# One more 128-column product per chunk in the weighted sum pass of a graph network kernel

## What is computed

```python
msgs = x[edge_src] * edge_val[:, None]
agg = jax.ops.segment_sum(msgs, edge_dst, num_segments=x.shape[0])
return agg @ weight
...
x = x + _L1_gnn_ref(_layernorm(x, axis=-1), src, dst, edge_weight, L1_gnn_weight)
```

## Time and profile before

| | us |
|---|---|
| median of 3 runs | 4542.22 |
| lowest and highest | 4536.57, 4546.24 |
| span of the profiled execution | 4528.2 |
| TensorE matmul busy in it | 3398.2 (75%) |
| POOL busy | 2322.5 (51%) |
| DVE busy | 2037.4 (45%) |
| ACT busy | 1546.8 (34%) |

### The profile page before, as it was taken

The page is one execution under the profiler, slowest core; times in us unless marked ns, Lnnn a source line. Parts: engine busy times, 40 slices in busy tenths (PEclk is TensorE's granted clock), DMA queues, the critical chain, the costliest instruction groups (busy, mean ns, idle before and its releaser), DMA issues. The chain is left out here.

```text
span 4528.2 us, 63030 instructions
## 1 busy us (share of the span) xinstructions
PE 3398.2 (75%) x18888; PEld 2727.4 (60%) x18888; DVE 2037.4 (45%) x5783; ACT 1546.8 (34%) x4091; POOL 2322.5 (51%) x2298
## 2 busy tenths in 40 slices
PE   3777887614396777774577199999778999998796
PEld 3555555412164555553466199998436888887696
DVE  4666555650144444342422311113445777777523
ACT  3554555310132222221322122222125666665432
POOL 3454555447405565554466543442336877875153
PEclk7788888756697887786789599999789999999698
DMA  6765555100005666661355377775549999997476
GB/s 188 217 168 149 153 159 146 53 22 3 0 24 191 223 226 212 205 219 49 94 166 157 101 243 246 248 235 165 142 150 244 268 261 268 266 265 188 136 214 206
DMA packets 491983, 777.53 MB, mean 172 GB/s; under 512 B 154330, under 2 KB 296995, under 8 KB 491395
## 3 DMA queue, kind: packets, MB, share of 16 engines
q1 hardware_dynamic: 359986, 498.14, 35.0%
q0 software_dynamic: 122608, 266.94, 23.8%
q10 hardware_dynamic: 9056, 8.43, 0.6%
HBM read 599.88 MB, written 173.38 MB: 171 GB/s over the span
## 5 line engine op out<-in xcount | busy, mean ns | idle before, releaser
L875 POOL DMA_INDIRECT sum_rows<-t_row,src_i x416 | 394.5, 948 | 441.1 <-POOLq L2144 161.2
L875 POOL DMA_INDIRECT ag_rows<-t_att,src_i x416 | 401.2, 964 | 372.9 <-DVE ag_msg L986 253.8
L1746 POOL DMA_INDIRECT eg_early<-t_edge,src_i x312 | 486.6, 1560 | 167.0 <-issue 90.2
L286 POOL DMA_INDIRECT t_cells<-times_seen,cell x416 | 405.5, 975 | 263.9 <-issue 126.7
L1066 PE MATMUL ps<-featT,ag_msg 128*128 128x128 f32 x1664 | 365.6, 353 | 131.8 <-issue 117.8
L1794 PE MATMUL ps<-eg_w,eg_rT 128*128 128x256 f32 x1664 | 434.4, 384 | 0.0
L1066 PEld LDWEIGHTS ps<-featT,ag_msg 128*128 128x128 f32 x1664 | 275.4, 236 | 232.2 <-issue 187.7
L1114 PE MATMUL ps<-sum_w1g,sum_eaT 64*128 64x256 f32 x1248 | 242.0, 521 | 203.7 <-ACT sum_kept L1158 117.8
L1473 PE MATMUL ps<-cv_cells,cv_high 128*128 128x384 f32 (+2 forms) x1200 | 323.2, 350 | 91.4 <-DMA cv_cells<-t_cells 91.4
L972 DVE TENSOR_TENSOR att_sums<-att_sums,ps 128x384 f32 x416 | 228.6, 550 | 310.7 <-remote 128.9
L1177 DVE TENSOR_TENSOR featT<-featT,ps 128x256 f32 x416 | 175.3, 421 | 401.4 <-remote 230.1
(11 more groups left out here) (446 smaller groups left out, 6746.8 us busy)
## 6 DMA issues: line engine op xcount, KB each, us to landing
cv_cells<-t_cells SPq DMA_DIRECT2D x225, 384.0 KB
t_pre<-sum_kept SPq DMA_DIRECT2D x156, 512.0 KB
eg_early<-t_pre SPq DMA_DIRECT2D x156, 512.0 KB
t_cells<-zeros SPq DMA_DIRECT2D x21, 1664.0 KB
cv_cells<-t_cells SPq DMA_DIRECT2D x75, 448.0 KB
xn<-in_L_ffn_W SPq DMA_DIRECT2D x57, 512.0 KB
xn<-in_L_ffn_expert_w SPq DMA_DIRECT2D x110, 256.0 KB
ag_trow<-t_dst SPq DMA_DIRECT2D x104, 256.0 KB
```

The lines of the kernel that those rows point to most:

```text
L286: nc.gpsimd.indirect_dma_start(out=t_cells, out_offset=bass.IndirectOffsetOnAxis(ap=cell[:, c:c + 1], axis=0), in_=times_seen[:, c:c + 1], ...
L875: nc.gpsimd.indirect_dma_start(out=rows[:, j, :], out_offset=None, in_=table, in_offset=bass.IndirectOffsetOnAxis(ap=src_i[:, n:n + 1], ax ...
L1746: nc.gpsimd.indirect_dma_start(out=early[:, q % ES, n % 2, :], out_offset=None, in_=t_edge, in_offset=bass.IndirectOffsetOnAxis(ap=src_i[: ...
```

## The change

Behind the three waits of a chunk and ahead of its two products, TensorE forms one more product: the identity (`ident`, 128x128 float32, already in SBUF) with itself, into columns 256 to 383 of the same PSUM bank. Nothing reads these columns. It waits for nothing of its own and increments no semaphore.

```diff
                         if n >= BANKS:
                             pe.wait_ge(g.added.sem, g.added.at(1 + n - BANKS + 1))
+                        nc.tensor.matmul(ps[:, n % BANKS, KD * EC:(KD + 1) * EC], ident[:], ident[:], start=True, stop=True)
                         for k in range(KD):
                             lhs = rows[:, j, k * 128:(k + 1) * 128]
                             mm = nc.tensor.matmul(ps[:, n % BANKS, k * EC:(k + 1) * EC], lhs, hot[:, j, :], start=True, stop=True)
```

## The result

The changed kernel takes 4575.4 us, the kernel before 4541.0 us (medians of five runs each). The ratio is 1.0065, with a 95% interval of 1.004 to 1.009: slower, by about 30 us. One of its five runs took 4977.8 us at a much lower granted clock (0.69 where the others had 0.85) and is left out of the ratio. A second set of runs of the same two kernels gave 1.0051 (1.0026 to 1.0076), some 23 us. The forecast was 4587 us, +45 us.

What follows compares the result with a forecast made beforehand. The weighted sum pass was taken as held by the loop TensorE, ACT, TensorE and TensorE's speed; 1.76 us added less 0.85 us saved a period, over 52 periods, taken as +45 us, gave 4587 us; range 4435 to 4670 us.

Steps and rivals of the forecast that it cites:

- What bounds the pass: Weighted sum pass, 685 us: held by the loop TensorE, ACT, TensorE and by TensorE's speed inside it; no engine full.
- POOL's floor: Weighted sum pass: POOL starts a gather every 1.25 us at best, 520 us for 416 chunks.
- The price of a product: Each extra product on TensorE: 0.22 us at the upper clock, 0.43 us at the lower; 93 to 177 us for all.
- The standstill: TensorE's 3.4 us rest per eight-chunk period, awaiting the ACT copy: some 0.45 us shorter, clock still falling after most.
- The lower stretch: The 6.0 us at half clock per period: +0.86 us of products; a sooner end saves 0.85 us, half the possible saving.
- The sum: Weighted sum pass: 1.76 us added less 0.85 us saved a period, times 52 periods, taken as +45 us.
- The checks named: Signs of the likeliest case: pass 700 to 760 us, mean clock 0.80 to 0.90, lower stretches nearer 3.4 than 6.8 us.
- slices 12 to 17: Profile page's slices, of 40, filled by the weighted sum pass; granted clock read there as 0.6 to 0.8.
- B: Rival: extra products fill TensorE's rests, so the clock stays up; 4444 us (4398 to 4489), -98 us; chance 0.32.
- C: Rival: clock pattern unchanged, products only add time to the pass; +91 us, 4633 us (to 4720); chance 0.17.
- D: Rival: products fall into TensorE's 188 us of rests, nothing measurable; 4542 us; chance 0.05.
- The 56 ns: Skill's spacing of 128-column matmul starts on the warm clock: 23 us for 416 products; the forecast used the rows instead.

Runs made afterwards that it cites:

- two_sets: Kernel before, no extra product: attribute products alternate between two bank sets, TensorE waits for the copy before the last, chunks have four banks, not six; ratio 0.9913.

## Why the prediction came out right, and where its steps did not

The forecast of +45 us had the sign right and the size within its range, in part by luck: the terms of its sum came out otherwise, and what they measured would by themselves have made about -10 us.

- *What bounds the pass.* TensorE, ACT and back, with TensorE's speed inside it: two_sets shows the loop, and two products against one show the clock. POOL's floor of 520 us was right as a floor but is never near; even without the loop the pass takes 610 us.
- *The price of a product.* 832 records came as foreseen. Recorded busy time grew by 39 us in the first pair of profiles and by 69 us in the second, less than 93 to 177 us. At the recorded spacing, 0.11 us for 728 of them and 0.21 us for the 104 at the lower clock, they cost 104 us. Against that fewer records ran at the lower clock, 536 and 580 of 3744 after, 991 and 765 of 2912 before, and some 40 us less were spent in rests.
- *The standstill.* This step failed. It said that each standstill gets 0.45 us shorter, to about 3 us, and that the clock falls after most of them. In its place there are fewer and longer ones: 29 rests of over 1 us instead of 53, 5.3 us in the usual period instead of 3.4 us, and one every sixteen chunks. Why the product ahead of the standstill is now signalled 5.7 us late instead of 3.4 us stays open, like the late signals themselves.
- *The lower stretch.* This term was mis-sized. I took half of the possible saving, 0.85 us in eight chunks. The lower stretch went from 6.0 us in eight chunks to 4.6 us in sixteen, 3.7 us less in eight; the same work at the upper clock takes half, so some 1.85 us were saved, twice what I took. Together with the longer standstill the usual period comes to 1.68 us a chunk, as it was.
- *The sum.* +45 us was expected, +23 to +30 us measured, and about +19 us between the profiles' means. The term that was too small is the saving by the clock. What is left as a loss can't lie in the usual period: 26.8 us for sixteen chunks against twice 13.6 us would gain 10 us over 416 chunks. The traces show where it lies. The kernel before has stretches at a high clock with 1.30 to 1.41 us a chunk, which the sum took no account of: of 25 blocks of 16 chunks 5 in its first profile and 14 in its second take less than 1.55 us a chunk, while in each of the two profiles after only one does, and 23 take 1.55 to 1.75 us. The changed kernel loses those stretches and repeats its one period almost throughout. Why it does is not shown by a run.
- *The checks named.* The clock was to lie between 0.80 and 0.90 (it is 0.88) and the pass between 700 and 760 us (693 and 701: at the edge). The lower stretches were to be nearer 3.4 than 6.8 us; they are, with 4.6 us.
- *Readings of the rows.* One profile was taken for the kernel: its second profile has a pass 27 us shorter, with far fewer of the periods on which the sum rests. The clock of slices 12 to 17 is 0.7 to 0.8, not 0.6 to 0.8. The window taken for the attention pass cuts off its end; the pass is 789 us long, 1.90 us a chunk, with 8.0 records in each.
- *The rivals.* B needs a clock above 0.93; one product doesn't reach it and two do, so the mechanism exists and the change stops short of it. Even two products don't bring B's pass of under 640 us (659). By the Trainium skill ("TensorE: Matmul & The Clock Gate", part 1), activity releases the throttle; the traces agree in direction, 0.79, 0.88 and 0.98 with none, one and two products. C is out, since the clock moved. D is out by the interval.
- *The 56 ns of the Trainium skill ("TensorE: Matmul & The Clock Gate", part 2) for a matmul of 128 columns.* The trace disagrees for these float32 products: the two records of each start 0.11 us apart at the upper clock and 0.21 us at the lower, so 0.22 us a product from the rows was the price to plan with. The third product, where no clock is to be won, lengthens the pass by 0.09 us a chunk with more than half of it hidden in rests.

## What to carry to other kernels

Work added to keep TensorE's clock up is paid at once, and what the clock gives back can be less or more: here one product lost 0.6%, two gained 0.3% and three lost 0.7%, and the same instructions without the work lost 1.0%. Look first for the dependence that makes TensorE rest; giving the copy a second set of banks gained 0.9% and raised the clock to 0.88, from 0.79 and 0.81, with no added work. And profile the unchanged kernel twice before a difference between two traces is believed: the edited pass of one and the same kernel differed by 27 us from one execution to the next, more than the change is worth.

## What the runs showed that I had not expected

- The signal of a product can reach ACT or DVE 3 to 6 us after the end of its record. Copies over 1 us late are more frequent at the upper clock (53 of 83 against 11 of 73 in one profile, 52 of 106 against 8 of 50 in the other).
- At a clock of 0.98 without rests, 11 records a chunk took 1.54 us, some 0.24 us more than their spacing in bursts adds up to.
- An unedited pass varied between 782 and 814 us over thirteen profiles, and medians of the same kernel before were 4552, 4509 and 4511 us in three sets of runs. Only ratios within a set can be compared.
- A product with 16 moving columns, two records as well, costs a chunk the same 0.22 us at the upper clock as one with 128, and added more recorded busy time to the pass.
- The same kernel's pass can take 691 or 664 us, with 5 or 14 of its 25 blocks of 16 chunks under 1.55 us a chunk.
